# Decoder layer on one core: cross attention's outputs through VectorE's block transposes and a DMA

## The reference

```python
# 1. self attention (16 heads, linear attention with decay), then two layer norms
o = Y @ Wout.T + x;  n = layernorm(o) * ln_g + ln_b
x1 = layernorm(x + n)
# 2. cross attention over ctx_1024 (8, 1024, 256), 16 heads of 16
attn = softmax(einsum('bnhc,bmhc->bhnm', qh, kh) * 16 ** -0.5)
out = einsum('bhnm,bmhc->bnhc', attn, vh).reshape(B, QL, DIM)
x2 = layernorm(x1 + out @ Wo.T + bo)
# 3. experts: softmax over the tokens of each sequence, each of 32 experts takes its 8 best tokens
logits = x2 @ gate_w.T + gate_b;  probs = softmax(logits, axis=tokens)
vals, idx = top_k(probs per expert, 8)
# each expert's MLP (256 -> 1024 -> 256, gelu) works on its mixed tokens;
# its output is combined back by vals, and a last layer norm follows
```

## Time and profile before

| what | value |
|---|---|
| median of 3 runs | 1839.48 us (1838.58 to 1839.82) |
| profiled execution, its own time | 1839.74 us |
| its span in the trace | 1837.9 us |
| PE, DVE, ACT, POOL busy | 91%, 67%, 46%, 33% of the span |
| mean granted TensorE clock | 0.953 of full speed |
| first cross attention max product; last value product | 628.9 us; 1644.5 us |
| experts stage begins | about 1676 us |

### The profile page before, as it was taken

One profiled execution on the slowest core, in us unless ns is written; L12 is line 12 of the kernel. 1 busy time (PEld: TensorE's weight loads), 2 busy tenths in 40 slices (PEclk: granted clock), 3 DMA queues, 4 the chain that ended last, 5 costly groups with the idle time before them and its releaser, 6 DMA issues. The chain is left out here.

```text
span 1837.9 us, 48963 instructions
## 1 busy us (share of the span) xinstructions
PE 1678.5 (91%) x19924; PEld 806.8 (44%) x19924; DVE 1232.9 (67%) x2424; ACT 838.3 (46%) x1015; POOL 598.2 (33%) x970
## 2 busy tenths in 40 slices
PE   5999999999999699999999999999999999976564
PEld 3566666666665333343333433433433334223332
DVE  5767677677674777868778788788687787812005
ACT  2334344344333136655646565566556465651103
POOL 3545545645625536043043061250430420000002
PEclk8999999999999779999999999999999999987777
DMA  7000000000000221111202101112112024046995
GB/s 252 3 4 4 3 3 3 3 3 3 3 32 15 69 67 50 41 38 59 83 1 85 56 28 65 50 38 69 35 64 78 1 89 183 30 179 267 421 418 183
DMA packets 62205, 141.44 MB, mean 77 GB/s; under 512 B 11280, under 2 KB 34320, under 8 KB 54320
## 3 DMA queue, kind: packets, MB, share of 16 engines
q1 hardware_dynamic: 61520, 137.88, 20.6%
q10 hardware_dynamic: 480, 0.59, 0.1%
HBM read 92.43 MB, written 7.86 MB: 55 GB/s over the span
## 5 line engine op out<-in xcount | busy, mean ns | idle before, releaser
L1680 DVE TENSOR_REDUCE mx<-cpsV 128x1 f32<-128x512 f32 x1024 | 655.2, 686 | 187.5 <-PE cpsV L1398 175.3
L1586 ACT ACTIVATE w<-cpsA 128x1024 f32<-128x1024 f32 x512 | 496.3, 1021 | 246.0 <-PE cpsA L1459 240.8
L1398 PE MATMUL cpsV<-w 96*128 96x512 bf16 x1024 | 325.4, 394 | 21.6 <-DVEq L1663 13.0
L1459 PE MATMUL cpsA<-w 99*128 99x512 bf16 x1024 | 275.2, 382 | 22.4 <-DMA w<-nmT 10.1
L1420 PE MATMUL cacc<-w 128*32 128x512 f32 x2048 | 279.7, 607 | 0.4 <-ACT w L1586 0.4
L468 PE MATMUL psA<-w 128*128 128x512 f32 x512 | 257.0, 625 | 5.0 <-DVE WT L1102 1.8
L1398 PEld LDWEIGHTS cpsV<-w 96*128 96x128 bf16 x1024 | 86.1, 98 | 283.4 <-DVE mx L1680 197.0
L1648 POOL TENSOR_TENSOR crstd<-cmv,eps 128x4 f32<-128x4 f32 x8 | 1.6, 202 | 605.8 <-DVE cmv L1746 605.8
L765 ACT COPY w<-psA 128x1024 f32<-128x1024 f32 x64 | 64.8, 1012 | 229.3 <-PE psA L468 229.3
L1459 PEld LDWEIGHTS cpsA<-w 99*128 99x128 bf16 x1024 | 93.0, 98 | 163.0 <-ACT w L1564 15.8
L885 POOL TENSOR_TENSOR VP<-V,VPF 128x128 f32<-128x128 f32 (+2 forms) x256 | 129.2, 535 | 42.7 <-PE psA L481 36.8
(11 more groups left out here) (224 smaller groups left out, 2227.6 us busy)
## 6 DMA issues: line engine op xcount, KB each, us to landing
w<-in_w SPq DMA_DIRECT2D x56, 1024.0 KB, 16.3
w<-w SPq DMA_DIRECT2D x189, 128.0 KB, 2.3
w<-w SPq DMA_DIRECT2D x189, 64.0 KB, 2.0
w<-in_ctxT SPq DMA_DIRECT2D x8, 1024.0 KB, 5.0
w<-in_xT SPq DMA_DIRECT2D x8, 512.0 KB, 6.4
x_tok<-in_x SPq DMA_DIRECT2D x8, 512.0 KB, 9.7
w<-in_w SPq DMA_DIRECT2D x8, 512.0 KB, 17.2
out_y<-w SPq DMA_DIRECT2D x16, 256.0 KB, 2.3
```

What stands on the lines that cost most here:

```text
L1398: nc.tensor.matmul(out, Qst[q // 2][0:ROWS, hh, g * P:(g + 1) * P], Kst[q // 2][0:ROWS, hh, half * BANK:(half + 1) * BANK], start=True, st ...
L1459: last = nc.tensor.matmul(out[:, n * T:(n + 1) * T], Kst[q // 2][0:ROWS + 3, hh, chunk * P:(chunk + 1) * P], Qst[q // 2][0:ROWS + 3, hh, : ...
L1586: nc.scalar.activation(Pr[:, (2 * s + pp) % 4, :], src, ACT.Exp, scale=CA_SCALE).then_inc(act_evac, 1)
L1680: nc.vector.tensor_reduce(mx[:, q % 2, row, k % 2:k % 2 + 1], full(m[k]), AX_X, ALU.max).then_inc(dve_evac, 1)
```

## The change

1. **Cross attention's outputs.** ScalarE's copy, both TensorE transposes, `O` and the `oT` evacuation go. VectorE transposes `cacc` in 32x32 blocks straight into `byq` at the end of the quad's last step (`take_outputs`), later divides there and transposes the blocks back into `byd` (`outputs`), and a DMA on SP's queue moves every second partition of `byd` to its rows of `oT` (`move_o`). V's columns are laid out interleaved for this (`0:2*HD:2`, ones at column 1). Quads 0 and 1 are divided in steps 12 and 20 of their sequence, quads 2 and 3 in step 1 of the next.
2. **Gate.** The gate product runs in step 11 as 128-token pieces on four column tiles, is biased into `L4` (128x128), and four DMAs move it to `L`; VectorE reads `L` in step 12.
3. **x2T** is transposed in two slots of `cpsA` (one for each half), the output projection takes two slots of `cpsV` and not four.
4. **Self attention's tail:** GpSimd adds `lnb` earlier, VectorE scales by `lng`.
5. **`keep_clock`** issues extra 128x128 transposes on TensorE in the tail: 34, 28, 6, 52 and 10.
6. SP's save of x2 moves ahead of the third `nmT`; `gate_b` is loaded by four DMAs.

```diff
-OUTPUTS, X1T, PROJECT_V1, PROJECT_Q, MERGE, PROJECT_O, NORM = 1, 0, 1, 4, 2, 4, 7
-PROJECT_K, X2T, COPY_X2, GATE, GATE_EXP, TOP8, TOP8_T, PICK, PICK_T = (7, 12), 9, 10, 12, 14, 20, 21, 28, 29
-PROJECT_V0 = 20
+X1T, PROJECT_V1, PROJECT_Q, PROJECT_O, NORM = 0, 1, 4, 4, 7
+PROJECT_K, X2T, COPY_X2, GATE, GATE_MAX, GATE_EXP, TOP8, TOP8_T, PICK, PICK_T = (7, 12), 9, 10, 11, 12, 14, 20, 21, 28, 29
+PROJECT_V0, LAST_OUTPUTS = 20, 27
...
                 def layer_norm_factors(r):
+                    if sec == "tail" and r == 0:
+                        pool.wait_ge(dve_evac, SA_DVE.count(sec, b, ("out", 1)) + DVE_SLOTS)
+                        add_lnb()
...
-                        dve.wait_ge(n1_scaled, b)
+                        if sec == "tail":
+                            dve.wait_ge(n1_ready, b * 2 - 1)
+                            nc.vector.tensor_tensor(n1[:], n1[:], lng[:].unsqueeze(1).broadcast_to([P, G, D]), ALU.mult)
+                            dve.drain()
+                        else:
+                            dve.wait_ge(n1_scaled, b)
...
+            def move_o(bb, q):
+
+                sp.wait_ge(o_ready, bb * QUADS + q + 1)
+                sp.dma_start(oT[64 * (q % 2):64 * (q % 2) + 64, q // 2, :], byd[q % 2][0:P:2]
+                             ).then_inc(o_moved[q % 2], 16)
...
+                if prev:
+                    if sec != "tail":
+                        move_o(b - 1, 2)
+                    move_o(b - 1, 3)
...
+                if prev:
+                    sp.wait_ge(l4_ready, b)
+                    for g in range(G):
+                        sp.dma_start(L[:, g * P:(g + 1) * P], L4[E * g:E * (g + 1)]).then_inc(l_moved, 16)
...
                     sp.dma_start(sh.p8_dram[:, bass.ds((b - 1) * T, T)], P8).then_inc(p8_saved, 16)
                 if now:
+                    move_o(b, 1)
                     if nxt:
                         stack_later(b + 1, 1, free=CA_ACT.count(sec, b, ("s", 16, 1)))
...
-                def o_transposes(bb, q):
-                    out = take_v(("otr", q))
-                    pe.wait_ge(acc_evac, bb * QUADS + q + 2)
-                    for g in range(G):
-                        last = nc.tensor.transpose(out[:, g * P:(g + 1) * P], OT[:, g * P:(g + 1) * P], sh.ident[:])
-                    last.then_inc(dve_full, 1)
+                def keep_clock(count):
+
+                    if sec == "tail":
+                        for _ in range(count):
+                            nc.tensor.transpose(acc[:, 0:P], sh.ident[:], sh.ident[:])
...
+                    if sec == "tail" and s == 1:
+                        pe.wait_ge(acc_evac, b * QUADS + 1)
+                        keep_clock(34)
                     if prev:
                         if s == PROJECT_O:
-                            evacuated_a("oT")
+                            for of in o_moved:
+                                pe.wait_ge(of, b * 32 + 16)
...
                             for k in range(KD):
-                                last = nc.tensor.matmul(out[0:E, :], gw[:, k, :], x2T[:, k, :],
-                                                        start=(k == 0), stop=(k == KD - 1))
+                                for g in range(G):
+                                    last = nc.tensor.matmul(out[E * g:E * (g + 1), 0:P], gw[:, k, :],
+                                                            x2T[:, k, g * P:(g + 1) * P], start=(k == 0), stop=(k == KD - 1))
...
+                def take_outputs(bb, q):
+
+                    dve.wait_ge(av_done, (bb * QUADS + q + 1) * KT)
+                    nc.vector.transpose(byq[q % 2][:].rearrange("p c s -> p (c s)"), acc[:]).then_inc(acc_evac, 1)
                     dve.drain()
+
+                def outputs(bb, q):
+
+                    t = byq[q % 2]
+                    nc.vector.reciprocal(rec[:], t[:, :, 1])
+                    dve.drain()
+                    nc.vector.tensor_tensor(t[:, :, 0:BLK:2], t[:, :, 0:BLK:2], rec[:].unsqueeze(2).broadcast_to([P, KT * 2, HD]),
+                                            ALU.mult)
+                    dve.drain()
+                    dve.wait_ge(o_moved[q % 2], bb * 32 + (q // 2 + 1) * 16)
+                    nc.vector.transpose(byd[q % 2][:], t[:].rearrange("p c s -> p (c s)")).then_inc(o_ready, 1)
+                    dve.drain()
...
+                    if now and s and s % KT == 0:
+                        take_outputs(b, s // KT - 1)
+                    if prev and s == 0:
+                        take_outputs(b - 1, 3)
```

More of the change, by code:

```diff
@@ L951, in body @@
                         level_logits()
-                    if i == 4 and prev:
+                    if i == 4 and prev and sec != "tail":
                         add_lnb()
@@ L957, in body @@
                         poly(*POOL_POLY[i])
-                    if i == 5 and prev:
+                    if i == 5 and prev and sec != "tail":
                         scale_by_lng()
@@ L1191, in ca_jobs @@
         if prev:
-            a += {MERGE: ["oT"], X2T: ["x2T"]}.get(s, [])
+            a += [("x2T", k) for k in range(KD) if s == X2T]
         if nxt:
@@ L1198, in ca_jobs @@
             v += m[0:2]
-        if s % KT == OUTPUTS and (now and s > KT or prev and s < KT):
-            v.append(("otr", (s // KT - 1) % QUADS))
         if prev:
-            v += [("wo", g) for g in range(G) if s == PROJECT_O]
+            v += [("wo", r) for r in range(2) if s == PROJECT_O]
             v += {GATE: ["lg"], TOP8_T: ["p8T"], PICK: ["mg"], PICK_T: ["mT"]}.get(s, [])
@@ L1503, in body @@
                             last.then_inc(dve_full, 1)
+                            keep_clock(10)
                     if now and s:
@@ L1513, in body @@
                         project_v(1)
[L1514 to L1516 removed]
                     if prev and s == X2T:
[L1518 to L1522 removed]
+                        for k in range(KD):
+                            out = take_a(("x2T", k))
+                            for g in range(G):
+                                if k == 0:
+                                    pe.wait_ge(x2_ready, (b - 1) * G + g + 1)
+                                last = nc.tensor.transpose(out[:, g * P:(g + 1) * P],
                                                            o2[:, g, k * P:(k + 1) * P], sh.ident[:])
[L1524 removed]
+                            last.then_inc(act_full, 1)
+                        keep_clock(6)
                     if nxt:
@@ L1590, in body @@
                     if prev:
-                        if s == MERGE:
-                            to_rows("oT", oT)
                         if s == X2T:
-                            to_rows("x2T", x2T)
+                            for k in range(KD):
+                                nc.scalar.copy(x2T[:, k, :], full(("x2T", k))[:, 0:T]).then_inc(act_evac, 1)
                         if s == COPY_X2 and sec != "mid":
@@ L1727, in body @@
                         max_jobs(s + LEAD, 0, 1)
-                    if s % KT == OUTPUTS and (now and s > KT or prev and s < KT):
-                        outputs((s // KT - 1) % QUADS)
+                    if prev and s == 1:
+                        if sec != "tail":
+                            outputs(b - 1, 2)
+                        outputs(b - 1, 3)
                     if prev:
@@ L1753, in body @@
                         if s == GATE:
-                            nc.vector.tensor_scalar(L[:], full("lg")[0:E, :], gb[:, 0:1], None, ALU.add
+                            nc.vector.tensor_scalar(L4[:], full("lg")[:, 0:P], gb[:, 0:1], None, ALU.add
                                                     ).then_inc(dve_evac, 1)
-                            dve.drain()
+                            dve.drain().then_inc(l4_ready, 1)
+                        if s == GATE_MAX:
+                            dve.wait_ge(l_moved, b * (16 * G))
+                            if now:
+                                outputs(b, 0)
                             nc.vector.max(m8[:], L[:])
@@ L1780, in body @@
                                                   ).then_inc(dve_evac, 1)
+                    if sec == "first" and s == GATE_MAX:
+                        outputs(b, 0)
+                    if now and s == TOP8:
+                        outputs(b, 1)
+                    if sec == "last" and s == LAST_OUTPUTS:
+                        outputs(b, 2)
                     if maxima:
```

97 lines of the change are left out of this document (44 added, 53 removed).

## The result

| kernel | median | range, executions | over the kernel before |
|---|---|---|---|
| before | 1839.65 us | 1838.58 to 1840.27, 4 | 1 |
| changed | 1854.86 us | 1852.11 to 1857.59, 4 | 1.0083 (95%: 1.0066 to 1.0101) |

The change costs 15 us. I had forecast 1844.4 us: slower, and for a reason that holds, but by less than a third of what it is, and the result lies outside my range (1825 to 1852). The profiled execution took 1856.31 us (span 1854.5), 16.6 more than before's.

The account below looks back on a forecast made before the run. TensorE was taken to bound cross attention (busy 96 of 100 us), weight DMAs after the tail's chain the last stage. Terms: -4.1 - 5.9 + 0.6 + 0.5 + 13.6 = +4.7, so 1844.4 us; range 1825 to 1852.

Parts of the forecast that it names:

- self attention's end: End of self attention: VectorE's two passes fall from 3.39 and 3.21 us without GpSimd's work beside them, -4.1 us.
- +0.5: Last sequence: savings of -1.33, -0.8, -0.2 against quad ends +0.6, uncovered step 12 +1.1, queue +1.6, last quad end -0.5.
- the projection starts at 1665.5: Tail: quad 3's move waits behind eight 1 MB weight DMAs, so the output projection starts there, not at 1650.49: +15.0 us.
- Rival A: Tail: quad 3's move is not held up by the weights; total -13.2, 1826.5 us; chance 0.18.
- The second transpose: Cross attention, step 2: the transpose goes with nothing in its place on TensorE, -1.33 us per sequence.
- The queue term: SP's queue, step 20: waiting for quad 1's outputs and one more DMA delay stack and `nmT` 1.5 us; +1.3 per sequence.
- Rival C: Cross attention: VectorE becomes the bound, 2 us per sequence lost beyond the sum, 1858 us; chance 0.08.
- Together per middle sequence ... -1.0: Cross attention: 0.8 - 1.33 - 0.8 - 0.2 - 1.0 + 0.25 + 1.3 = -1.0 us; six of them -5.9.
- the quad ends: Cross attention: VectorE's emptying of `cacc` loses the saved 0.52 us and 0.2 more; four per sequence, +0.8.
- the gate with VectorE's block: Cross attention, step 12: new gate form -1.0 us per sequence, VectorE's block lengthened by `outputs` of quad 0 +0.25.
- Rival B: Cross attention: `nmT` has slack and block transposes run at 0.62; 10 to 12 us gained, 1834 us; chance 0.12.
- net -1.4: Tail behind the projection's start: some 5.5 us off through extra transposes, against the four DMAs to `L` and 0.3 for the wider adds.

Follow-up runs that it names:

- e1: Kernel before with only self attention's tail changed (GpSimd adds lnb earlier, VectorE scales by lng): 1834.45 us, 0.9981 of before.
- e5: Changed kernel without the 130 extra transposes of `keep_clock` in the tail: 1858.09 us, 1.0097 of before.
- e2: Changed kernel with the last eight weight DMAs of cross attention issued behind the move of quad 3: 1846.99 us, 1.0049 of before.
- e3: Changed kernel with the tail's move of quad 3 and its four DMAs to `L` on ScalarE's queue: 1842.40 us, 1.0037 of before.
- e4: Changed kernel with the move of quad 1 issued behind the fourth quad's `nmT`, not ahead of the stack: 1843.69 us, 1.0032 of before.
- e12: Changed kernel with old gate, last eight weight loads behind quad 3's move, quad 1's move and last sequence's 4 MB behind `nmT`, without `keep_clock`: 1814.43 us, 0.9875 of before.
- e6: Changed kernel with the gate of before (one 32-row product, no DMAs to `L`) and 20 extra transposes after it, not 52: 1849.80 us, 1.0061 of before.
- e7: Changed kernel run again, unedited: 1856.41 us, 1.0091 of before.

## Why the prediction missed

Against the profiled execution it was off by 11.9 us (+16.6 and not +4.7). By its steps:

| step | forecast | measured | off by |
|---|---|---|---|
| self attention's end | -4.1 | -4.48 (e1: -3.5) | -0.4 |
| sequences 0 to 5 (0.6 and five times -1.0) | -4.4 | -0.46 | +3.9 |
| sequences 6 and 7 (-1.0 and +0.5) | -0.5 | +3.45 | +3.9 |
| last value product to first projection | +15.0 | +15.76 | +0.8 |
| projection to first expert product | -1.4 | +1.19 | +2.6 |
| experts | 0 | +1.1 | +1.1 |

**Right.** The step that decided, "the projection starts at 1665.5", holds within 1 us; e5's row names the move, and e2 and e3 show that what stands ahead of it in the queue is the cause. Rival A (the move isn't held) is out. The second transpose gave 1.33 a sequence to the hundredth. The queue term was sized right as a wait: the stack is 1.4 us later, where I had 1.5, TensorE's waits in step 24 of sequences 1 to 6 grew from 1.9 to 8.5 us, 6.6 against six times 1.3, and e4 shows that it is the order of SP's list. Rival C is out too: VectorE still waits 0.25 us for TensorE in a regular step (row 1096.72 above).

**Wrong, the middle sequences.** The step that failed is "Together per middle sequence ... -1.0". Its single terms are off, but nearly cancel: the quad ends cost +0.35 and not 0.8 (the block transpose's 0.71 was right, but 3.44 against 3.35 is 0.1 an end and not 0.2); the projection gave 0.5 and not 0.8 (16 products take 4.0 us to the next value product, I had put 3.7); x2T gave 0.37 and not 0.2 (4.16 to 3.79 us in its step); the gate with VectorE's block gave 0.5 (14.20 to 13.69 us over its steps) and not 0.75 (1.0 less the block's 0.25). What was missing is that a wait on TensorE can have a second price: the clock falls behind it, 1.7 us each time, here twice. These 3.4 us are most of the 3.9. The differences of sequences 0 to 5, one by one (-0.05, -0.56, -1.34, -0.16, +1.93 and -0.28 us), say the same: sequence 2, with a wait of 0.85 us and no fall, beats my -1.0, and sequence 4, with the pause of 2.25 us and the fall, is the one that loses. I priced every wait at its own length. e4 measures wait and clock together: 11.7 us in six sequences, where I had 1.3 for each of five. Rival B had this gain right in size (10 to 12), as one that the kernel would keep.

**Wrong, the last sequence.** I read +0.5 there. Eight weight loads also stand in front of `nmT` of quad 1 (issued 1549.61, TensorE released 1558.93), and step 8 waited 1.84 us (before 0.69). In step 12 nothing covers VectorE's block, which TensorE waited 3.46 us for (before 1.09; I had +1.1). Step 24 took 9.3 us (before 7.45; I had +1.6, which is right). The stretches at the lower clock around these lasted 3.4, 6.8 and 10.2 us, against 3.4 and 6.8 before.

**Wrong, the tail's chain.** The step that failed is "net -1.4" (its terms give -1.3): it came to +1.19 (+2.6 against e1, whose tail is before's and took 25.00 us from projection to experts, where before's profile has 26.41). The moves to `L` are not to blame; MAX8 waited 4.18 us for them, and I had 3.9. On the other side stood 5.5 us for the extra transposes. The first 34 were over at 1648.9, 16 us ahead of the projection, which ran at 5.69 us (6.26 before). The middle ones kept the clock up for the gate (0.64 us), but without them it took 1.08 (e5), against 3.59 before: the gate is short mostly by its new form, not by the clock. From the projection to the last small product they save 0.8 us in all (23.26 us, in e5 24.10). And the last ten, at the lower clock, stand in front of the stage's end, where I had put them at nothing: from the last small product to the first expert product it is 4.34 us with them and 2.48 without (e5; 2.49 before), 1.9 us lost. e5's time shows the sum of all 130 to be nothing here, e12's some 3 us for 98 where no move is held. The 1.1 us in the experts are within what profiles of an equal expert stage show (161.0 us before, 162.9 in e1).

How much of the tail's 3.5 us for the new gate (e6) is its DMAs, how much its wider bias and how much the 32 extra transposes was not tried. Part 6 of the change was not tried by itself either; none of TensorE's waits for `nmT` stands in step 16, where the save of x2 was moved.

## What to carry to other kernels

Before work is moved onto a DMA, look at what stands ahead of it in the same queue at every place where it will be issued, the rare ones (last sequence, tail) above all: here one issue place, behind 8 MB, cost 15 us, more than the new outputs save in all eight sequences. The order of issue is free and decides the sign: the new outputs are 15 us slower than before behind the weights and 26 us faster in front of them (there with the old gate), 14.6 of which a kernel with the old outputs and the weights behind `nmT` does not reach. A wait on TensorE can cost more than its length: add the low clock that may follow it.

## What the runs showed of the hardware

- A 128 KB move from SBUF to SBUF landed 2.5 us after its issue, 18.1 us with 8 MB of loads ahead of it on its queue, and 7.8 us with the same 8 MB on another queue.
- Issuing a DMA took SP 0.6 us mostly, but single ones 1 to 2.3 us, in the kernel before as well, and four small moves 2.5 to 3.4 us together.
- A block transpose of 128x512 took VectorE 0.72 us out of PSUM and 0.71 out of SBUF, at 1245 ns for 1024 columns.
- After a pause of 2.25 us in cross attention, TensorE's next products ran for 3.4 us at the lower clock; after one of 2.24 us in the same execution they did not. In the profiles of changed, e2, e3, e5, e6 and e7 ten of the twelve waits for `nmT` of 1.7 to 2.4 us in sequences 0 to 5 were followed by a fall, and none of the five of 1.3 to 1.6 us. Before, the pause of 1.13 us was not.
